# First attention: every second step's scores and maxima as 64-row products in the two halves of the array

## What is computed

```
x = x + attn_a(layernorm(x))          # 1 x 2048 x 128
Q = (x @ Wq.T + bq); K = (x @ Wk.T + bk); V = (x @ Wv.T + bv)   # 16 heads of 64
scores = einsum('bnhd,bmhd->bhnm', Q, K) * SCALE * adaptive_scale[h]
w = softmax(scores);  attn = einsum('bhnm,bmhd->bnhd', w, V)
y = x + (attn @ Wo.T + bo);  result = layernorm(y) * gamma + beta
```

## Time and profile before

| what | value |
|---|---|
| median of 3 runs | 1926.67 us (1925.68 to 1926.8) |
| span of the profiled execution | 1927.3 us |
| PE busy | 1854.3 us (96%), 23471 products |
| DVE busy | 1443.6 us (75%) |
| ACT busy | 1548.5 us (80%) |
| POOL busy | 1597.5 us (83%) |
| first attention's steps | 55.1 to 1197.2 us of the span |
| granted TensorE clock, mean | 0.987 |

### The profile page before, as it was taken

One profiled execution on the slowest core, in us unless ns is written; L12 is line 12 of the kernel. 1 busy time (PEld: TensorE's weight loads), 2 busy tenths in 40 slices (PEclk: granted clock), 3 DMA queues, 4 the chain that ended last, 5 costly groups with the idle time before them and its releaser, 6 DMA issues.

```text
span 1927.3 us, 55726 instructions
## 1 busy us (share of the span) xinstructions
PE 1854.3 (96%) x23471; PEld 1256.4 (65%) x23471; DVE 1443.6 (75%) x2647; ACT 1548.5 (80%) x1921; POOL 1597.5 (83%) x1025
## 2 busy tenths in 40 slices
PE   4899999999999999999999998779999999999998
PEld 3566666666666666666666665547777777767766
DVE  7798878878878878878878875566767767767652
ACT  4799999999999999999999999646666666666664
POOL 3899999999999999999999999358688787787752
PEclk8999999999999999999999999889999999999999
DMA  6101100100100100100100100100000000000000
GB/s 148 35 11 26 34 15 22 35 17 20 35 19 18 35 19 18 35 19 17 35 23 14 35 2 2 55 1 2 2 1 2 2 2 2 2 1 1 2 2 23
DMA packets 45034, 37.96 MB, mean 20 GB/s; under 512 B 8304, under 2 KB 44144, under 8 KB 44528
## 3 DMA queue, kind: packets, MB, share of 16 engines
q1 hardware_dynamic: 44304, 34.00, 7.0%
q10 hardware_dynamic: 480, 0.39, 0.1%
HBM read 8.15 MB, written 1.05 MB: 5 GB/s over the span
## 4 chain that ended last, share of the span: by engine, by line
PE 87%; DVE 4%; POOL 3%; issue 3%; ACT 2%; DMA 0%; SPq 0%; POOLq 0%; DVEq 0%; ACTq 0%
PE ST L1639 11%; PE ST L1640 11%; PE RING L1520 7%; PE OO L1601 6%; PE OO L1603 6%; PE OO L1600 6%; PE OO L1520 4%; PE ST L1832 3%; PE ST L1838 3%; PE ST L1837 3%; PE ST L1839 3%; POOL PBUF L704 2%; PE OO L1859 2%; PE OO L1861 2%; PE OO L1863 2%
## 5 line engine op out<-in xcount | busy, mean ns | idle before, releaser
L620 POOL TENSOR_TENSOR PAB<-PR,PAB 128x1024 f16<-128x1024 f32 x342 | 724.3, 2134 | 42.3 <-ACT PAB L799 42.2
L799 ACT ACTIVATE PAB<-ST,exp_scale 128x1024 f16<-128x1024 f32 x512 | 567.6, 1109 | 0.0
L1104 DVE TENSOR_REDUCE maxes<-RING 128x1 f32<-128x512 f32 x661 | 439.6, 684 | 122.6 <-PE RING L1520 118.2
L1600 PE MATMUL OO<-VP,PAB 128*128 128x66 f16 x4096 | 446.6, 192 | 2.9 <-POOL PAB L620 2.9
L1601 PE MATMUL OO<-VP,PAB 128*128 128x64 f16 x4096 | 447.1, 193 | 0.0
L1603 PE MATMUL OO<-VP,PAB 128*128 128x66 f16 x4096 | 445.1, 192 | 0.0
L797 ACT ACTIVATE PR<-ST,exp_scale 128x1024 f32<-128x1024 f32 x342 | 381.9, 1117 | 64.7 <-PE ST L1640 61.8
L1600 PEld LDWEIGHTS OO<-VP,PAB 128*128 128x128 f16 x4096 | 380.2, 96 | 78.3 <-issue 15.5
L1601 PEld LDWEIGHTS OO<-VP,PAB 128*128 128x128 f16 x4096 | 377.0, 97 | 60.6
L1639 PE MATMUL ST<-QL,KH 128*128 128x512 f16 x1024 | 388.6, 380 | 2.0 <-DVE QH L1116 1.0
L1640 PE MATMUL ST<-QH,KL 128*128 128x512 f16 x1024 | 388.8, 380 | 0.0
(11 more groups left out here) (319 smaller groups left out, 4027.8 us busy)
## 6 DMA issues: line engine op xcount, KB each, us to landing
KH<-HS SPq DMA_DIRECT2D x124, 64.0 KB, 2.0
QL<-HS SPq DMA_DIRECT2D x64, 64.0 KB, 2.0
QL<-LS SPq DMA_DIRECT2D x64, 64.0 KB, 2.0
QH<-HS SPq DMA_DIRECT2D x64, 64.0 KB, 2.0
KL<-LS SPq DMA_DIRECT2D x62, 64.0 KB, 2.0
X<-in_L_attn_a_x SPq DMA_DIRECT2D x4, 256.0 KB, 4.2
SHARED<-in_rope_cos SPq DMA_DIRECT2D x1, 1024.0 KB, 5.2
SHARED<-in_rope_sin SPq DMA_DIRECT2D x1, 1024.0 KB, 7.3
```

The lines of the kernel that those rows point to most:

```text
L620: pool.tensor_tensor(PB[:, s, :], PRA[g % PR_SLOTS], PA[:, s, :], ALU.subtract).then_inc(p_low_ready, 1)
L799: act.activation(PA[:, step % SLOTS_A, :], ST[step % 2][:, :], ACT.Exp, scale=scale).then_inc(sa.exps, 1)
L1104: dve.reduce_max(maxes[:, i // BLOCKS, i % BLOCKS:i % BLOCKS + 1], bank[:, :], X_AXIS).then_inc(sa.ring_taken, 1)
L1600: pe.matmul(o, high, v[:, 0:V2_AT], start=(m == 0 and qt == 0), stop=False, skip_group_check=True)
```

## The change

Even steps get a form of their own, `scores_in_halves_a`. The scores of key tile 0 are made of four 64-row products in the upper half of the array (rows 64 to 127), those of key tile 1 of four in the lower half. Four maxima, two in either half, are put between them; each uses q high alone against k high, 64 rows, where it was q high and q low before (the row's maximum only has to be near). Products of different halves write different PSUM banks. Odd steps keep their undivided score products and have no maxima. Some operands are needed in the other half too: q low of the unit's block in the lower half and the row maxima in the upper one stand in a new tile `QX` (two buffers), k low of every second key tile in the lower half of `KL16` as well.

```
-HEAD_STEPS = (0, 4)
-MOVES = 6
+HEAD_STEPS = (1, 5)
+QUERY_MOVES, KEY_MOVES = 3, 4
...
-    ahead, at = (1, 2 * step + 4) if step < 6 else (2, 2 * step - 12)
+    ahead, at = (1, 2 * step + 4) if step < 6 else (2, 0)
...
-    if not (last and ul + ahead >= UNITS_A):
-        items += [("max", ahead, at), ("max", ahead, at + 1)]
+    if step % 2 == 0 and not (last and ul + ahead >= UNITS_A):
+        items += [("max", ahead, at + i) for i in range(4)]
...
+                             (KL16[hs][0:DA, q.start + P:q.start + 2 * P], low[DA:P, P:2 * P])):
...
+                if g % STEPS_A == 0 and g + STEPS_A < ITER_A * G_A:
+                    nhead, nqb = divmod(g // STEPS_A + 1, BLOCKS)
+                    wait(sp, sa.scores, g + 1)
+                    sp.wait_ge(parts_moved[nqb], (nhead * MOVES + QUERY_MOVES) * 16)
+                    sp.dma_start(QX[0:DA, (nqb) % 2, :], QL16[nhead % 2][DA:P, nqb * BLK:(nqb + 1) * BLK]
+                                 ).then_inc(qx_moved, 16)
...
+            def take_rows_a(bank, item, unit):
+
+                head, qb = divmod(unit, BLOCKS)
+                dve.wait_ge(sa.ring_put, item + 1)
+                rows = bank[0:BT, 0:P].unsqueeze(1).broadcast_to((BT, BT, P))
+                for dst in (QH16[head % 2][0:BT, qb * BLK:(qb + 1) * BLK], QX[DA:DA + BT, unit % 2, :]):
+                    ins = dve.scalar_tensor_tensor(dst.rearrange("p (a c) -> p a c", c=P), rows,
+                                                   lifts[0:BT, head:head + 1], rowmask[:, :, :], ALU.add, ALU.mult)
+                ins.then_inc(sa.ring_taken, 1)
...
+            def scores_in_halves_a(g, maxima):
...
+                kh0, kl0, kh1, kl1 = (KH16[hs][upper, keys0], KL16[hs][upper, keys0],
+                                      KH16[hs][lower, keys1], KL16[hs][lower, keys1])
+                qh0, ql0, rows0 = QH16[hs][upper, q], QL16[hs][upper, q], QX[upper, u % 2, :]
+                qh1, ql1, rows1 = QL16[hs][lower, q], QX[lower, u % 2, :], QH16[hs][lower, q]
...
+                if step == 0:
+                    pe.wait_ge(qx_moved, (u + 1) * 16)
+                maximum(0, QL16, lower)
+                maximum(1, QH16, upper)
+                wait(pe, sa.exps, g - 1)
+                pe.matmul(tile0, kh0, qh0, start=True, stop=False)
+                pe.matmul(tile1, kh1, qh1, start=True, stop=False)
+                pe.matmul(tile0, kl0, qh0, start=False, stop=False)
+                pe.matmul(tile1, kl1, qh1, start=False, stop=False)
+                pe.matmul(tile0, kh0, ql0, start=False, stop=False)
+                maximum(2, QL16, lower)
+                pe.matmul(tile0, row_units[upper, :], rows0, start=False, stop=True)
+                pe.matmul(tile1, row_units[lower, :], rows1, start=False, stop=False)
+                pe.matmul(tile1, kh1, ql1, start=False, stop=True).then_inc(sa.scores, 1)
+                maximum(3, QH16, upper)
```

More of the change, by code:

```diff
@@ L973, in _ @@
             dve.memset(ones_f[:, :], 1.0).then_inc(const_r, 1)
+            link(dve.memset(row_units[:, :], 0.0))
+            for at in (0, DA):
+                dve.memset(row_units[at:at + BT, :], ROW_UNIT)
+            dve.memset(QX[DA:P, :, :], 0.0)
             for i in range(2):
@@ L1073, in take_projected_a @@
                 if head > 0:
[L1074 to L1075 removed]
+                    dve.wait_ge(keys_lead[blk], KEY_MOVES * 16)
+                    dve.wait_ge(parts_moved[blk], (head * MOVES - KEY_MOVES) * 16)
                 bias = QKB[:, head:head + 1]
@@ L1515, in max_a @@
                     for moved in parts_moved:
-                        pe.wait_ge(moved, (head * MOVES + 3) * 16)
+                        pe.wait_ge(moved, (head * MOVES + QUERY_MOVES) * 16)
                 claim_a(item)
@@ L1641, in scores_a, with maximum @@
                 ins.then_inc(sa.scores, 1)
+            def scores_in_halves_a(g, maxima):
+                u, step = divmod(g, STEPS_A)
+                head, qb = divmod(u, BLOCKS)
+                hs = head % 2
+                q = slice(qb * BLK, (qb + 1) * BLK)
+                lower, upper = slice(0, DA), slice(DA, P)
+                keys0, keys1 = (slice((2 * step + j) * P, (2 * step + j + 1) * P) for j in range(2))
+                tile0, tile1 = (ST[step % 2][:, j * BLK:(j + 1) * BLK] for j in range(2))
+                kh0, kl0, kh1, kl1 = (KH16[hs][upper, keys0], KL16[hs][upper, keys0],
+                                      KH16[hs][lower, keys1], KL16[hs][lower, keys1])
+                qh0, ql0, rows0 = QH16[hs][upper, q], QL16[hs][upper, q], QX[upper, u % 2, :]
+                qh1, ql1, rows1 = QL16[hs][lower, q], QX[lower, u % 2, :], QH16[hs][lower, q]
+                def maximum(place, queries, half):
+                    if not maxima:
+                        return
+                    item, (_, ahead, i) = maxima[place]
+                    mhead, mqb = divmod(u + ahead, BLOCKS)
+                    if i == 0 and mqb == 0:
+                        for moved in parts_moved:
+                            pe.wait_ge(moved, (mhead * MOVES + QUERY_MOVES) * 16)
+                    qt, c = divmod(i, BLOCKS)
+                    at = mqb * BLK + qt * P
+                    claim_a(item)
+                    pe.matmul(RING3[item % 3][:, :], queries[mhead % 2][half, at:at + P],
+                              KH16[mhead % 2][half, c * BLK:(c + 1) * BLK], start=True, stop=True
+                              ).then_inc(sa.ring_put, 1)
+                if step == 0:
[13 more added lines that the diff above has]
+                maximum(3, QH16, upper)
@@ L1670, in _ @@
                     pe.wait_ge(sa.ring_taken, rows_item + 1)
-                if g != 1:
+                items = ITEMS_A[g]
+                beside = []
+                if step % 2 == 0:
+                    beside = [] if g == 0 else [(n, item) for n, item in items if item[0] == "max"]
+                    scores_in_halves_a(g, beside)
+                elif g != 1:
                     scores_a(g)
@@ L1678, in _ @@
                             max_a(1, i, MAX_LEAD[i])
-                items = ITEMS_A[g]
                 before = sum(item[0] == "max" for n, item in items)
-                for n, item in items[:before]:
+                for n, item in items[len(beside):before]:
                     ring_item_a(n, item, u)
```

20 lines of the change are left out of this document (11 added, 9 removed).

## The result

The changed kernel takes **2034.31 us** (median of 4 runs, 2032.63 to 2036.58); the kernel before, timed beside it, 1926.74 us (1925.68 to 1928.29). The ratio is 1.0553, with a 95% interval of 1.0540 to 1.0567: 107.6 us slower. The forecast was 1992 us, +65, with a range of 1940 to 2060. The sign and the main mechanism came out as forecast; 42 us of the size did not, and most of them belong to a cost that the forecast had set to nothing.

The account below looks back on a forecast made before the run. PE bounds the kernel (busy 96%), with POOL's floor at 133.8 of 142.8 us a cycle. PE's 129.0 plus 21.5 of waits plus 1.1 gives 151.6 a cycle, +65 us after the last head's deduction: 1992 us, range 1940 to 2060.

Parts of the forecast that it names:

- A pair shares a slot: Even steps on PE: two 64-row products in different halves take one 0.216 us slot, saving 13.8 us a cycle.
- Rival 3: Even steps: the halves don't run together, giving twelve slots and about 2160 us; chance 0.05.
- The ring: Even steps' four maxima: PE, at most three items ahead, waits for DVE; all waits together 21.5 us a cycle.
- behind projects: Even step after a project: third and fourth maxima wait for DVE, 0.94 us each time, 7.5 us a cycle.
- in light even steps: Even steps with no other item before them: only the fourth maximum waits, 0.05 us each, 0.8 a cycle.
- at the quotients: PE's first product into O waits for DVE's division behind four reductions, 0.55 us each, 4.4 a cycle.
- at the row maxima: Next unit's first step waits for DVE to write row maxima to two places, 0.50 us each, 2.0 a cycle.
- Rival 2: ACT's and POOL's lead swallows half or more of PE's waits for DVE: 1902 us, or 1855 at best; chance 0.12.
- The change of the array's division: Switching PE between undivided array and halves, twice each even step: taken at 0, upper bound 0.16 us a change.
- Rival 1: Row tiles drain the array at changes of division, 0.16 us each: 54 us more, 2046 us; chance 0.20.
- POOL's floor: Unit without project, values or turned item stays at POOL's 16.7 us, adding 1.1 us a cycle.
- The last head: The last head prepares no next one, so its project and values waits fall away: 5.6 us off.

Follow-up runs that it names:

- the second: Kernel before, old order, every maximum a 64-row product in the lower half, q low's part left out: 2033.63 us, ratio 1.0547.
- the third experiment: Kernel before, old order, each step's two maxima as 64-row products, one in each half, q low's part left out: 1931.26 us, ratio 1.0018.
- the last one, with the same balance: Changed kernel with scores in halves kept but maxima spread over every step, project and values at steps 0 and 4: 1944.95 us, ratio 1.0091.

## Why the prediction was right, and where its size was off

- **A pair shares a slot: right.** Starts 3 ns apart in the median, 0.216 us from pair to pair (0.226 from the first to the second), and 102 us between the second and the third experiment. The saving of 13.8 us a cycle is real. Rival 3 falls. The Trainium skill (TensorE: Matmul & The Clock Gate, "Measured speedup vs the span model") gives 3.07x for four row tiles and about 4 ns for each further tile; for two tiles the 3 ns of this trace agree.
- **The ring gives back more than the halves save: right.** A burst without halves costs 178.5 us, and undoing the pieces of the order gives 99.5 back, with the row maxima 112.8. PE's starts in the six like cycles give each term of the sum, in us a cycle: 7.0 behind projects (forecast 7.5), 3.0 behind values (3.7), 2.9 behind turned items (3.1), 1.5 in light even steps (0.8), 4.1 at the quotients (4.4), 1.4 at the row maxima (2.0). Together that is 20.0, unrounded, against 21.5. Rival 2, that the waits are swallowed, falls: 20.0 is above its 13.8, and PE waits for neither ACT nor POOL in these cycles, so every wait is paid in full. (The forecast calls the item that M2 needs "two places before M0"; it is the one right before M0, and the forecast's sums use that one.)
- **The change of the array's division, taken at 0: wrong; this is the term that was mis-sized.** It measured 0.197 us an even step, 6.3 us a cycle, 50 us in all. The reasoning that failed was the choice of the nearest row: the row maxima's transposition has all its rows and four output columns, and that is free in the changed kernel too. Half the rows is not. The profile gives only `128*4` for it; that it runs in a 32-column tile, and so changes the division at all, no trace shows. The upper bound, the tail of 0.16 us each way, was not reached either: 0.094 in and 0.103 out. Rival 1 thus had the right kind of price at 0.6 of its size; its sign, a gap at either end of every even step, is in the trace beside all the signs of the forecast, and its 2046 us is nearer to the 2034 measured than the forecast's 1992. That 2034 lies within the stated range is owed to the range being drawn around rival 1 as well, and not to the forecast's own sum. The Trainium skill (TensorEngine Tiling (Array Packing), "Key Properties") says that changing the mode drains the engine: for rows the trace bears out that something is paid, though less than the tail of the last product; for columns the trace contradicts it only if the transposition is such a tile. Since the profile's ends of products are modelled, it can't show whether the array is ever empty.
- **POOL's floor: taken at 1.1, measured 0.** The forecast let the one unit without project, values or turned items stand at POOL's 16.7 us and charged PE with the difference. POOL's starts do keep that distance, but PE does not stand for POOL there, before or after: POOL lags behind PE by a changing amount, and only the whole cycle counts.
- **The sum for a cycle.** 142.7 before - 13.8 slots + 6.3 division + 20.0 waits = 155.2, measured 155.8. The last 0.6 is two hundredths in each even step, one from the first to the second pair and one at the first product with V. The forecast had 151.6: its waits and floor were 2.6 too many, the division and these hundredths 6.9 too few.
- **The last head and the first.** The forecast took 5.6 us off because the last head prepares no next one. Against the 13.1 us by which a like cycle grew, the last one grew by 8.1, so 4.9 came off. The first cycle grew by 17.0, 4.0 more, which the forecast did not have. At five places between 118 and 158 us DVE works ahead of the reduction of M0 for the second attention, once in the whole run, and M3 waits for that too:

```profile
117.86 1.21 DVE L1159 TENSOR_REDUCE b_sums<-PBUF 128x8 f32<-128x1024 f32 x1
118.98 0.68 DVE L1119 TENSOR_REDUCE maxes<-RING 128x1 f32<-128x512 f32 x1
119.72 0.39 PE L1692 MATMUL RING<-KH,QH 64*128 64x512 f16 x1 [0.91 <-DVE maxes L1119]
```

- **The lead.** "At most 1 us" for constants moved to DVE; the first subtraction comes 3.2 us later. The other eight traces don't allow that to be put on this edit: the three kernels without it have their first subtraction at 57.95 to 58.25 us (56.27 before), and the five others with it at 57.41 to 59.75. What it costs stays open.
- **The DMAs taken at nothing** cost nothing that shows: among the 60 longest waits within the first attention none is for a DMA.
- Together: 17.0 + 6 x 13.06 + 8.1 = 103.5 for the stretch, + 3.2 of lead - 1.6 behind it = 105.1 us, the difference of the spans; the medians stand 107.6 apart. Of the forecast's 65 us the division makes it 50 more and the waits it overrated 21 less; the remaining 11 or so are the hundredths, the first cycle and the lead.
- **Of what would show it**, the idle time before M2 and M3, at the quotient and the pairs are in the trace as named. POOL is busy 86% of the stretch (89 forecast), since the stretch is longer. "No gap of 0.16 us at the change of division" holds to the letter, but there is one of 0.1.

## What to carry to other kernels

Before work is bunched to save slots on one engine, ask who frees the buffers that it fills: with a ring of three and a consumer of 0.6 us an item, four items at once wait for what was put in before them, so that another item of the ring belongs right behind the burst and not right ahead of it. Count what entering and leaving a special form of the array costs and compare it with the slots saved between the two: here 0.2 us for 0.43 in the changed kernel, and 0.2 for 0.215, which is nothing, in the third experiment; the last one, with the same balance, lost by its waits. Look also at work that the buffers' consumer does only once: behind a burst it is paid for in full. And when a faster order comes out slower, move the consumers' work before giving it up: all of the 107.6 us lost came back, and 5.7 more, by four edits that change no product.

## What the hardware did that was not expected

- A change between undivided products and 64-row tiles costs 0.092 to 0.103 us in either direction (512-column and 66-column neighbours alike), about half of what a product of 512 columns stands apart from the next, and with no semaphore in play. A transposition of four output columns with all rows costs no more than an undivided one: it stands 0.03 us behind the product before it and 0.11 ahead of the next.
- Two 64-row products in one half, one after the other, stand 0.226 us apart right behind a change into halves and 0.216 later on, undivided ones 0.216; so half the rows alone save nothing.
